# The third group of turned probability blocks leaves PSUM through ScalarE instead of VectorE

## What is computed

```
x = x + layernorm(attention(layernorm(x)))   # 16 query heads, 4 key/value heads, width 64, rope, causal
x = x + layernorm(ffn(layernorm(x)))         # linear, swiglu, mixture of 8 experts (top 4) + shared, linear, swiglu

scores = einsum('bkgqd,bkpd->bkgqp', q, k) * 64 ** -0.5
scores = where(causal, scores, -1e30)
out = einsum('bkgqp,bkpd->bkgqd', softmax(scores), v)
```

## Time and profile before

| | |
|---|---|
| median of 3 runs | 1497.17 us (1492.41 to 1498.75) |
| profiled execution | 1495.59 us, its span 1493.6 us |
| TensorE busy | 1337.3 us, 90% of the span |
| VectorE busy | 1004.2 us, 67% |
| ScalarE busy | 777.9 us, 52% |
| GpSimd busy | 393.8 us, 26% |
| mean granted TensorE clock | 0.981 |

### The profile page before, as it was taken

The page is one execution under the profiler, slowest core; times in us unless marked ns, Lnnn a source line. Parts: engine busy times, 40 slices in busy tenths (PEclk is TensorE's granted clock), DMA queues, the critical chain, the costliest instruction groups (busy, mean ns, idle before and its releaser), DMA issues.

```text
span 1493.6 us, 30981 instructions
## 1 busy us (share of the span) xinstructions
PE 1337.3 (90%) x10432; PEld 936.3 (63%) x10432; DVE 1004.2 (67%) x2056; ACT 777.9 (52%) x1706; POOL 393.8 (26%) x388
## 2 busy tenths in 40 slices
PE   2699999988999998799999988999999899999996
PEld 1477777675777676676677676777776644444442
DVE  3577777836777788377777864777768367666664
ACT  2566665535665655365666544566655333333332
POOL 0344353013353521153433212433531000000000
PEclk9899999999999999999999999999999999999997
DMA  8212111011111110111121011121110000000000
GB/s 234 82 37 75 56 53 67 2 43 68 58 53 67 35 61 15 64 55 63 33 74 56 25 44 58 31 75 56 53 57 1 1 0 7 8 7 8 8 7 15
DMA packets 79027, 67.63 MB, mean 45 GB/s; under 512 B 39904, under 2 KB 62304, under 8 KB 78816
## 3 DMA queue, kind: packets, MB, share of 16 engines
q1 hardware_dynamic: 78944, 66.55, 13.7%
HBM read 7.81 MB, written 2.10 MB: 7 GB/s over the span
## 4 chain that ended last, share of the span: by engine, by line
PE 63%; DVE 15%; issue 12%; ACT 6%; SPq 2%; DVEq 1%; DMA 0%; ACTq 0%; POOL 0%; POOLq 0%
PE o_out L466 13%; PE rows L417 13%; PE turn L436 8%; PE rows L603 7%; DVE neg_max L1036 6%; ACT probs L708 5%; PE o_out L626 3%; PE rows L420 3%; PE proj_bank L436 3%; DVE ql L1028 2%; PE o_out L387 2%; PE proj_bank L387 1%; DVE probs L1157 1%; PE proj_bank L370 1%; PE proj_bank L372 1%
## 5 line engine op out<-in xcount | busy, mean ns | idle before, releaser
L1036 DVE TENSOR_REDUCE neg_max<-rows 128x1 f32<-128x768 f32 (+7 forms) x512 | 362.7, 749 | 251.2 <-PE rows L420 251.0
L708 ACT ACTIVATE probs<-rows,neg_max 128x768 f32<-128x768 f32 (+7 forms) x512 | 374.8, 737 | 251.5 <-DVE neg_max L1036 249.1
L466 PE MATMUL o_out<-probsT,v_g 128*64 128x128 f32 (+1 forms) x3328 | 279.1, 318 | 0.7 <-DVE probsT L1050 0.7
L466 PEld LDWEIGHTS o_out<-probsT,v_g 128*64 128x64 f32 x3328 | 201.8, 137 | 69.0 <-issue 19.1
L417 PE MATMUL rows<-kk,qh 64*128 64x512 f32 (+2 forms) x768 | 169.8, 438 | 83.3 <-ACT probs L708 75.4
L436 PE MATMUL turn<-cf,probs 128*128 128x128 f32 x1792 | 242.0, 275 | 0.8 <-DVE probsT L1050 0.7
L717 ACT ACTIVATE probsT<-turn 128x512 f32<-128x512 f32 x256 | 152.6, 596 | 165.3 <-PE turn L436 154.6
L904 POOL COPY inv_wide<-inv_sum 128x256 f32<-128x256 f32 x128 | 50.9, 398 | 706.1 <-DVE inv_sum L1042 697.9
L436 PEld LDWEIGHTS turn<-cf,probs 128*128 128x128 f32 x1792 | 194.4, 142 | 2.4 <-issue 1.0
L417 PEld LDWEIGHTS rows<-kk,qh 64*128 64x128 f32 x768 | 73.2, 187 | 166.2 <-ACT probs L708 133.6
L1050 DVE COPY probsT<-turn 128x512 f32<-128x512 f32 x256 | 171.4, 669 | 3.0 <-PE turn L436 2.5
(11 more groups left out here) (154 smaller groups left out, 1728.1 us busy)
## 6 DMA issues: line engine op xcount, KB each, us to landing
turned<-raw SPq DMA_DIRECT2D x192, 128.0 KB, 2.0
v_g<-v_all SPq DMA_DIRECT2D x32, 256.0 KB, 3.0
kk<-kk SPq DMA_DIRECT2D x16, 512.0 KB, 2.9
kl<-kl SPq DMA_DIRECT2D x16, 512.0 KB, 3.7
slab_a<-w_qk SPq DMA_DIRECT2D x16, 256.0 KB, 2.6
xm<-in_x SPq DMA_DIRECT2D x4, 512.0 KB, 7.3
slab_b<-w_qk SPq DMA_DIRECT2D x16, 128.0 KB, 2.2
out<-xm SPq DMA_DIRECT2D x8, 256.0 KB, 2.3
```

What stands on the lines that cost most here:

```text
L466: ins = mm(dst, v_g[p][:, t, :], x, start=t == 0, stop=t == big_w - 1)
L708: A(probs[:, s % 2, q * 128:q * 128 + width], rows[h][:, 0:width], ACT.Exp, bias=neg_max[:, s % 2, item:item + 1], accum_out=exp_sum[:, s ...
L1036: V.tensor_reduce(neg_max[:, s % 2, item:item + 1], rows[h][:, 0:width], AX_X, ALU.max, negate=True).then_inc(max_ready, 1)
```

## The change

Group 2 moves from VectorE to ScalarE. `BY_ACT` becomes (0, 2, 4) and `BY_DVE` (1, 3), so the semaphores' counts follow. In each step VectorE no longer copies group 2 between group 1 and the output product. ScalarE copies it behind its two big exponentials and ahead of `keep_high`. At a batch boundary ScalarE takes groups 0, 2 and 4 behind its second, third and fourth projection copy (before: 0 and 4 behind the second and fourth). Nothing is changed on TensorE, GpSimd or SyncE.

```
-BY_ACT, BY_DVE = (0, 4), (1, 2, 3)
+BY_ACT, BY_DVE = (0, 2, 4), (1, 3)
@@ ScalarE, step
                 exponentials(b, g, s, 1)
+                if depth > 0:
+                    keep_turned(b, *at, 2)
                 for ahead, k in rope_plan(s, 2, last):
                     keep_high(b, g + ahead, k)
@@ ScalarE, prologue
                     keep_raw(b, 0, k, rows[k % 2][:, k // 2 * HALF:k // 2 * HALF + HALF])
-                    if b and k in (1, 3):
-                        keep_turned(*at, BY_ACT[k // 2])
+                    if b and k:
+                        keep_turned(*at, BY_ACT[k - 1])
@@ VectorE, attend
                     keep_turned(b, g1, s1, 1)
-                    keep_turned(b, g1, s1, 2)
@@ VectorE, drain
                 keep_outputs(b, HKV - 1, STEPS_G - 2)
-                keep_turned(*at, 2)
                 keep_turned(*at, 3)
```

## The result

| | before | after |
|---|---|---|
| median, 4 runs each | 1496.28 us | 1516.95 us (1513.06 to 1519.31) |
| ratio after / before | | 1.0148, 95% interval 1.0127 to 1.0168 |
| profiled execution | 1495.59 us, span 1493.6 | 1516.15 us, span 1514.1 |

What follows compares the result with a forecast made beforehand. The prediction took TensorE's stream, plus the places where TensorE waits for another engine's chain, as the bound. Crossings 20.6, last head groups +1.5, batch boundaries -1.2 made 20.9 us on 1497.2: 1518 us, range 1510 to 1528.

Steps and rivals of the forecast that it cites:

- Relief of VectorE at nothing: 128 group 2 copies of 0.68 us leave VectorE; taken at 0 in the steps, because TensorE's output matmuls hide it.
- The rounding moves by 0.48: ScalarE's rounding of one roped half (keep_high), queued behind the moved copy, moves by 0.48 us in every step having one.
- The subtraction crosses the product in places 4 and 5: Steps 4, 5 of a head group (0 to 7): VectorE's low subtraction starts 0.33, 0.23 us behind GpSimd's sine product.
- The price of a crossing: TensorE loses 0.60 us per place-4 step and 1.12 per place-5 step, twelve of each: 20.6 us.
- Places 2, 3, 6 and 7 at 0: Steps at these places lose 0: subtraction already blocked in 2, 3, 6; in 7 it waits for L1064 longer than 0.48.
- Last head groups +1.5, boundaries -1.2: Last head group of each batch: place 3 loses 0.37, 1.5 us in four; three batch boundaries gain 0.4 each, 1.2.
- Only one place crosses: Rival: only place 5's subtraction falls behind the product; 13.4 + 0.3, so 1511 us; chance 0.04.
- Everything late is paid: Rival: slack in places 4 and 5 hides nothing, TensorE pays all lateness; 29.8 + 0.3, 1527 us; chance 0.06.
- Shift without blocking: Rival: subtraction behind the product keeps its short time; place 5 loses 2.4 us, 1500 us in all; chance 0.12.
- The faster rival: Rival: VectorE's shorter queue puts the subtraction ahead of the product in places 2 and 6; 36 us gained, 1461; chance 0.04.

Runs made afterwards that it cites:

- e3: Kernel before with the group 2 copy left out altogether, no TensorE wait for it, its buffer cleared once by GpSimd: 1495.45 us, ratio 1.0006.
- e1: Changed kernel, but ScalarE copies group 2 behind keep_high instead of ahead of it: 1494.38 us, ratio 1.0006 to the kernel before.
- e2: Kernel before, group 2 still on VectorE, plus a spare unread 384-column ScalarE copy ahead of keep_high: 1516.36 us, ratio 1.0158.
- e6: Changed kernel plus a GpSimd wait: the sine product starts only after the previous item's low subtraction ends; 1465.23 us, ratio 0.9802 to the kernel before.
- e5: Kernel before plus a GpSimd wait: the sine product starts only after the previous item's low subtraction ends; 1457.29 us, ratio 0.9761.
- e8: Kernel before plus a spare unread 128-column ScalarE copy ahead of keep_high: ratio 1.0041 to the kernel before.

## Why the prediction was right, point by point

*Relief of VectorE at nothing:* right, shown twice. e3 gives the relief alone and measures 1.0006, and after the change the output product's wait grew by 70.5 of the 87 us.

*The rounding moves by 0.48:* right, 0.47 in the trace of after.

*The subtraction crosses the product in places 4 and 5, in all 24 steps:* right. The waits after name 24 subtractions of the `kl` half held by the rounding (10.2 us), and the mean of 1323 ns over 32 is what 24 long and 8 short ones make: (12 x 1.48 + 12 x 1.59 + 8 x 0.69) / 32 = 1.32. That the crossing is the cause, and not the load or the moved copy, is shown from three sides: the copy without the delay loses nothing (e1), the delay without the copy loses everything (e2), and with the order held the change loses 8 and not 21 (e6).

*The price of a crossing:* a little too low. Forecast 0.60 and 1.12 for TensorE, measured 0.69 and 1.22. I moved the start of the lower scores and left their speed alone. The start came out as forecast: 447.52 less the 7.45 by which this step lies later is 440.07. But behind the wait their first matmul takes 0.50, where the one that ran straight on behind the upper scores took 0.39; that is the missing 0.1. It is not the wait as such: in the kernel before, small scores at 237.11 take 0.50 too, with no idle time, behind the output matmuls. With 12 x (0.69 + 1.22) = 22.9 the attention part should lose 23.2. The order of time has the same instruction at the end of attention, in before and then in after:

```profile
1161.42 2.13 DVE L970 TENSOR_SCALAR attn_out<-attn_out,mean_var,rstd 128x128 f32<-128x128 f32 x8
```

```profile
1184.80 2.13 DVE L972 TENSOR_SCALAR attn_out<-attn_out,mean_var,rstd 128x128 f32<-128x128 f32 x8
```

That is 23.4, with eight stretches of low clock in each of the two traces from the first step on. The spans differ by 20.5 only, since the last 90 us of the feed-forward part, which the change does not touch, ran 2.9 shorter in the profile of after, at a granted clock of 0.98 and not 0.92. Before, then after:

```profile
1400.00:1493.60 93.60, 78.62 (x213) 35.11 (x211) 52.73 (x148) 32.88 (x53) 0.00 (x0) 0.92 0.04 12
```

```profile
1423.40:1514.10 90.70, 75.46 (x209) 34.31 (x211) 52.75 (x148) 32.86 (x53) 0.00 (x0) 0.98 0.04 12
```

So the forecast's 20.9 met the median's 20.7 partly by luck: the price was 2.3 too low. The interval of the ratio, 19 to 25 us, holds both.

*Places 2, 3, 6 and 7 at 0:* right; the place-6 wait of TensorE is 1.54 after as before.

*Last head groups +1.5, boundaries -1.2:* seen in the steps' lengths, 0.38 in place 3 of four groups and -0.39 at the first boundary (41.72 to 41.33, from the last step's big maxima to the next batch's first, both at a granted clock of 0.96; at the other two the clocks differ). Too small for any timed run.

*Only one place crosses* did not happen. *Everything late is paid* holds for place 5 (1.22 of its 1.23) and not for place 4, where TensorE's slack hid its part: 0.69 of 1.25.

*Shift without blocking:* its price was 5 too low by the medians (3 forecast, 7.9 measured between e5 and e6). Of that place 5 makes 1.4 (0.12 more in each, mostly the same 0.1 in the first lower score matmul), and place 2 of the last head groups 0.6; the rest is not taken apart, and the clock is part of it.

*The faster rival:* wrong in what could bring it, and in its price. VectorE's shorter queue hardly ever lets the subtraction start ahead of the product: in e3 it does in 2 of the 36 steps of places 2, 3 and 6, in the kernel before in 1. Taking the product out of its way does it in all (e5). The price was put at TensorE's whole idle time, 24 x 1.5 = 36; places 2 and 6 gave back 0.95 and 0.92 each, some 22 us, since TensorE still waits 0.61 there. That e5's 37 lies near the 36 is luck: the rest comes from place 3, the last head groups and what the last section says.

## What to carry to other kernels

Where VectorE and GpSimd both read two tensors from SBUF, look in the order of time at which of the two starts first and by how much; if the margin is a tenth of a microsecond and the VectorE one is on a path to TensorE, every edit ahead of either can cost or give a microsecond per step. Don't leave that order to chance: one semaphore wait on the engine with the slack fixed it here for 37 us. And when work is moved to an idle engine, put it behind what somebody waits for on that engine, not ahead of it; two exchanged lines were 21 us.

## What the runs showed of the hardware

*The late subtraction ends 0.55 us behind the product, whether it starts 0.06 or 0.35 us behind it.* Starts behind the product of 0.06, 0.17, 0.24, 0.35 us gave durations of 1.77, 1.67, 1.59, 1.48: the sum is 1.83 to 1.84 each time, the product's 1.28 and 0.55. So the product's end sets the subtraction's, and the subtraction's own start does not. (GpSimd's times are rough by the profile's own legend; that the sum is the same to 0.01 at four different starts speaks for them here.) And the product is held by an earlier subtraction: 1.74 to 1.78 in place of 1.28 (444.55 in the earlier trace rows, 450.58 in e8). This is what "SBUF — State Buffer" in the Trainium skill states in "Who interferes with whom"; the 0.55 is less than the subtraction's own 0.68.

*The granted clock drops for short stretches during attention.* I had not looked for it. In the kernel before, TensorE idles 1.62 ahead of the lower scores at 230.95, and about a microsecond later it runs at half of full speed, the lower of its two levels (1.2 and 2.4 GHz):

```profile
230.95 0.50 PE L417 MATMUL rows<-kk,qh 64*128 64x512 f32 x2 [1.62 <-ACT probs L708]
```

By stretches, columns: busy time of PE, PEld, DVE, ACT, POOL, granted clock, DMA share, GB/s:

```profile
231.00:232.00 1.00, 1.00 (x9) 0.59 (x10) 0.00 (x0) 0.39 (x1) 0.00 (x0) 1.00 0.00 0
232.00:233.00 1.00, 1.00 (x8) 1.00 (x7) 0.89 (x2) 0.00 (x0) 0.00 (x0) 0.51 0.00 0
233.00:234.00 1.00, 1.00 (x6) 1.00 (x6) 0.87 (x3) 0.90 (x2) 0.00 (x0) 0.50 0.00 0
234.00:235.00 1.00, 1.00 (x6) 0.59 (x6) 0.84 (x2) 1.00 (x3) 0.40 (x1) 0.50 0.00 0
235.00:236.00 1.00, 1.00 (x10) 0.60 (x8) 0.42 (x1) 0.77 (x3) 0.00 (x0) 0.79 0.00 0
```

That step took 9.55 us where its like take 7.93. In e5, whose place-6 wait is 0.61, all twelve place-7 steps take 7.93; in the kernel before two take 9.55, one 8.79, and the place-6 step ahead of that one 9.43. These make 5.0 us; two batch boundaries with such a drop (granted clock 0.96, and 1.00 in e5) make 2.9, and e5 has one drop early in the first batch that costs it 1.6. So from the first step's maxima to the last one's the two traces differ by 33.1 for the orders and 6.3 for the clock, 39.4 us.

But this execution of e5 is the fastest of its five, at a mean granted clock of 0.989; the others took 3.4 to 6.1 us longer at 0.983 or 0.984, and the kernel before had 0.980 to 0.985. So the clock's part in the median's 37 us is smaller than in the traces. The orders' 33 are shown step by step and lie at the lower end of the interval of 33 to 38; the other 4 of the median are not taken apart.

In e6 such a drop lies at each of the three batch boundaries, where e5 has none. The one of the second:

```profile
578.00:580.00 2.00, 2.00 (x7) 1.52 (x6) 1.97 (x6) 1.19 (x2) 0.00 (x0) 0.50 0.02 7
```

Why a drop follows this idle stretch and not another of 1.63 one head group earlier, or those of 1.54 beside it, was not tried and stays open.
